# Two graph layers on one core: gathers for padding left out, and the subtraction of the means moved to GpSimd

## What is computed

```python
def layer0(x, src, dst):
    msg = concatenate([x[dst], x[src] - x[dst]])
    h = leaky_relu(msg @ W1 + b1, 0.01)
    h = leaky_relu(h @ W2 + b2, 0.01)
    return segment_sum(h, dst)

def layer1(x, src, dst):          # with a loop at every node
    y = (x @ W).reshape(N, 4, 64)
    logits = leaky_relu(sum(y * att_src)[src] + sum(y * att_dst)[dst], 0.2)
    alpha = softmax of logits over the edges of one dst
    return segment_sum(y[src] * alpha, dst).mean(heads) + bias

x = layernorm(x + layer0(x, src, dst))
x = layernorm(x + layer1(x, src, dst))
```

## Time and profile before

| | |
|---|---|
| median of 3 runs | 8135.93 us (8133.81 to 8150.75) |
| profiled execution | 8149.11 us |
| its span, first to last instruction | 8147.3 us |
| mean granted TensorE clock | 0.894 |
| busy: PE, DVE, ACT, POOL | 5916.5, 5650.8, 3861.1, 5850.7 us |
| gathers of the first layer | 3088, starts 95.1 to 3951.2 us |
| norm and set-up between the layers | 3978 to 4066 us |
| gathers of the second layer | 3087, starts 4043.6 to 7917.4 us |
| last turn's end, end of the last norm | 8031, 8147 us |

### The profile page before, as it was taken

The page is one execution under the profiler, slowest core; times in us unless marked ns, Lnnn a source line. Parts: engine busy times, 40 slices in busy tenths (PEclk is TensorE's granted clock), DMA queues, the critical chain, the costliest instruction groups (busy, mean ns, idle before and its releaser), DMA issues.

```text
span 8147.3 us, 248848 instructions
## 1 busy us (share of the span) xinstructions
PE 5916.5 (73%) x46847; PEld 4536.0 (56%) x46848; DVE 5650.8 (69%) x13519; ACT 3861.1 (47%) x10093; POOL 5850.7 (72%) x6184
## 2 busy tenths in 40 slices
PE   6787788777778877877546666666666766767667
PEld 5555565555555655555435555555555555555556
DVE  5555555555555555555658888888888888888887
ACT  4444444444444444444324545444454544545443
POOL 4777777777777777777477777777777777777760
PEclk8999999999989999999778889888888988888887
DMA  4222222222222222222211111111111111111120
GB/s 112 41 41 41 41 41 42 42 41 41 41 41 41 41 42 41 42 41 41 36 32 31 32 32 31 32 31 32 31 32 32 31 32 31 32 32 31 32 27 17
DMA packets 299581, 306.84 MB, mean 38 GB/s; under 512 B 193032, under 2 KB 196726, under 8 KB 298632
## 3 DMA queue, kind: packets, MB, share of 16 engines
q0 software_dynamic: 197600, 261.23, 18.2%
q1 hardware_dynamic: 99476, 38.71, 2.1%
q10 hardware_dynamic: 2068, 3.20, 0.1%
HBM read 286.38 MB, written 16.30 MB: 37 GB/s over the span
## 4 chain that ended last, share of the span: by engine, by line
POOL 28%; issue 23%; PE 22%; DVE 9%; SPq 9%; DVEq 4%; ACT 2%; POOLq 2%; DMA 2%; ACTq 0%
POOL big L492 28%; PE pu L1093 9%; SPq L377 5%; PE ps L975 2%; PE pu L989 2%; SPq L373 2%; ACT ST L1213 2%; PE ps L1012 2%; PE pu L1023 2%; PE ps L1007 2%; POOLq L480 1%; DVE state L822 1%; DVE ps L764 1%; DVE Y L793 1%; DVEq L271 1%
## 5 line engine op out<-in xcount | busy, mean ns | idle before, releaser
L492 POOL DMA_INDIRECT big<-x_dram,idx x3087 | 2933.7, 950 | 1032.5 <-issue 1026.1
L492 POOL DMA_INDIRECT big<-q_dram,idx x3088 | 2916.0, 944 | 1034.3 <-issue 1027.0
L1093 PE MATMUL pu<-Y,S 128*128 128x265 f32 x7872 | 2305.4, 441 | 1059.3 <-DVE state L822 1057.6
L1093 PEld LDWEIGHTS pu<-Y,S 128*128 128x128 f32 x7872 | 1590.7, 213 | 1418.3 <-issue 1139.6
L793 DVE TENSOR_TENSOR Y<-big,ps 128x1040 f32<-128x1040 f32 x984 | 1214.7, 1234 | 387.9 <-PE pu L1093 280.0
L596 DVE TENSOR_TENSOR S<-ps,few 128x1024 f32 x978 | 1197.9, 1225 | 168.1 <-DVE few L591 123.8
L636 DVE TENSOR_TENSOR ps<-ps,rowX 128x512 f32<-128x512 f32 x491 | 343.6, 700 | 1320.6 <-ACT rowX L1224 1318.5
L1213 ACT COPY ST<-ps 128x1024 bf16<-128x1024 bf16 x489 | 494.9, 1012 | 1277.6 <-PE ps L975 1226.2
L989 PE MATMUL pu<-rowX,S 128*128 128x192 bf16 x3936 | 555.6, 268 | 445.7 <-SPq L397 400.0
L1296 ACT COPY ST<-ps 128x1024 bf16<-128x1024 bf16 x490 | 495.4, 1011 | 637.6 <-PE ps L1116 600.7
L989 PEld LDWEIGHTS pu<-rowX,S 128*128 x3936 | 382.0, 99 | 603.0 <-issue 515.0
(11 more groups left out here) (179 smaller groups left out, 8267.8 us busy)
## 6 DMA issues: line engine op xcount, KB each, us to landing
big<-x_dram SPq DMA_DIRECT2D x6272, 0.3 KB
big<-q_dram SPq DMA_DIRECT2D x6144, 0.4 KB
big<-q_dram,idx POOLq DMA_INDIRECT x3088
big<-x_dram,idx POOLq DMA_INDIRECT x3087
rowX<-flag_dram SPq DMA_DIRECT2D x196, 32.0 KB
x_dram<-big SPq DMA_DIRECT2D x7, 483.0 KB, 6.8
idx<-srcT_dram SPq DMA_DIRECT2D x98, 32.0 KB
dstc<-dstT_dram SPq DMA_DIRECT2D x98, 32.0 KB
```

Source lines behind the costliest of these rows:

```text
L492: nc.gpsimd.indirect_dma_start(o, None, x_dram if l else q_dram, bass.IndirectOffsetOnAxis(ap=idx[:, half, t:t + 1], axis=0)).then_inc(gat ...
L1093: last = t_.matmul(bank, Sf[:, t, :], Y[:, t, :], start=(t == 0), stop=(t == 7))
```

## The change

The turns are counted without the group of padding (STEPS is 488). In the last batch all engines run 7 groups and not 8, and GpSimd gathers 53 tiles and not 64 (in the second layer one of them is SP's); VectorE and SP wait for so many. `supers` can leave more than the last batch outside its loop, since VectorE has to know in the batch before which number to wait for: VectorE's last 3 batches of the second layer are now written out.

In the norm between the layers VectorE forms the mean and GpSimd subtracts it. VectorE forms three means ahead and not one: its order is now centre of c+2, spreads of c, logits of c-1, scale of c. The last norm stays as it was.

```diff
-STEPS = G + NB - 1
+STEPS = NG + NB - 1
+REST = NT - (NS - 1) * TS
+GREST = -(-REST // TG)
...
-        def supers(eng, body):
-
-            with eng.Fori(0, NS // 2) as q:
+        def supers(eng, body, rolled=NS // 2 * 2):
+
+            with eng.Fori(0, rolled // 2) as q:
                 body(q * 2, q, 0)
                 body(q * 2 + 1, q, 1)
-            if NS % 2:
-                body(NS - 1, NS // 2, 0)
+            for i in range(rolled, NS):
+                body(i, i // 2, i % 2)
+
+        def final(i):
+
+            return isinstance(i, int) and i == NS - 1
...
-                with self.eng.Fori(0, GS if between is None else GS - 1) as r:
+                with self.eng.Fori(0, GREST if final(i) else GS if between is None else GS - 1) as r:
                     self.group(l, i, r, turn, arrive)
...
             for l in range(2):
+                if l:
+                    for c in range(NCH):
+                        pool.wait_ge(meaned, c + 1)
+                        y = x0[:, c * BC:(c + 1) * BC, :]
+                        mm = mean[:, c * BC:(c + 1) * BC]
+                        nc.gpsimd.tensor_tensor(y, y, mm.unsqueeze(2).to_broadcast([P, BC, D]), ALU.subtract
+                                                ).then_inc(centred, 1)
...
-                    for r in range(GS):
+                    for r in range(GREST if final(i) else GS):
                         pool.wait_ge(L[l]["y1" if l else "z1"], free)
...
-                        for t in range(r * TG, r * TG + TG):
+                        for t in range(r * TG, min(r * TG + TG, REST) if final(i) else r * TG + TG):
...
                 link(v.tensor_reduce(mm, y, AX.X, ALU.add))
+                if base == 0:
+                    v.tensor_scalar(mm, mm, 1.0 / D, None, ALU.mult).then_inc(meaned, 1)
+                    return
...
-            centre(chunk_of(x0, 0), 0, 0)
+            for c in range(3):
+                centre(chunk_of(x0, c), c, 0)
             for c in range(NCH):
-                if c + 1 < NCH:
-                    centre(chunk_of(x0, c + 1), c + 1, 0)
+                if 3 <= c + 2 < NCH:
+                    centre(chunk_of(x0, c + 2), c + 2, 0)
                 spreads(c, 0)
...
-                dve.wait_ge(gath[half], q * (16 * (TS - 1)) + 16 * (TS - 1))
+                dve.wait_ge(gath[half], q * (16 * (TS - 1)) + 16 * ((REST if final(i) else TS) - 1))
...
-            supers(dve, steps1)
+            supers(dve, steps1, (NS - 2) // 2 * 2)
```

More of the change, by code:

```diff
@@ L232, in build @@
         sgp, sgv = sem("sg_pe"), sem("sg_dve")
+        meaned = sem("ln_meaned")
         centred, squared, spread, rooted, normed = [sem(f"ln_{n}") for n in "centred squared spread rooted normed".split()]
@@ L395, in landed @@
                         n = TG - 1
+                    if final(i):
+                        n = min(TG, REST - r * TG)
                     sp.wait_ge(slot[half][r], q * (16 * (TG if r < GS - 1 else TG - 1)) + 16 * n)
@@ L424, in chunk1 @@
                 sp.dma_start(idx[:, half, :], srcT_dram[:, ds(i * TS, TS)]).then_inc(idx_in[half], 16)
-                if not (isinstance(i, int) and i == NS - 1):
+                if not final(i):
                     row_numbers(1, i + 1, 1 - half)
@@ L878, in steps1 @@
                 dve.wait_ge(dst_in[half], (q + 1 + (NS - NS // 2 if half == 0 else NS // 2)) * 16)
-                last = isinstance(i, int) and i == NS - 1
+                last = final(i)
                 walk1.steps(1, i, turn1(half), between=None if last else lambda: arrived(i + 1, q + half, 1 - half))
@@ L1124, in steps1 @@
                 turn_maxima(i)
-                walk1.steps(1, i, turn, between=None if isinstance(i, int) and i == NS - 1 else lambda: turn_logits(i + 1))
+                walk1.steps(1, i, turn, between=None if final(i) else lambda: turn_logits(i + 1))
             prime(pe, 1, "stp ad U0 U1")
```

## The result

The changed kernel takes 8114.5 us, the median of 7 runs (8100.3 to 8119.4); beside it the kernel before took 8135.6 (7 runs, 8133.8 to 8150.8). The ratio is 0.9961, with a 95% interval of 0.9952 to 0.9970, which is 24 to 39 us less. The two medians are only 21.1 us apart, and that lies outside the interval. In a second session before had a median of 8144.4 in 21 runs and the changed kernel one of 8116.5, ratio 0.9959 (0.9945 to 0.9973), and these medians are 27.9 us apart. The profiled execution has a span of 8117.6 us against 8147.3, 29.7 us less.

The account below looks back on a forecast made before the run. GpSimd's gather list was taken to bound each layer, with VectorE's turns after the last batch; -17.5 + 0.6 - 4.8 - 1.8 - 6.4 = -29.9 us off the median 8135.9 gave 8106 us, range 8096 to 8122.

Parts of the forecast that it names:

- Part 1: End of first layer: 11 gathers fewer and PE taking the last real group earlier, -17.5 us (bounds -13.7 and -18.5).
- Part 2: Norm between the layers: start later by GpSimd's 2.0 us subtractions, +0.6 us; VectorE's relief counted as 0.
- Part 3: Second layer's last batch: VectorE's 4.78 us wait for gathers goes, -4.8 us, and a cold PE with it, -1.8 us.
- The cold PE: Second layer, behind the last batch's wait: first accumulation takes 2.06 us instead of 3.90, -1.8 us (bounds 0 and -2.1).
- Part 4: Second layer's last turns: one turn less, -6.4 us.
- Part 5: VectorE's last three batches of the second layer written out instead of one: 0, bounds -1 and +3 us.
- The signs: Trace checks, among them second layer's gathers starting 14 to 18 us earlier, VectorE waiting 2.6 us for PE, rounds 6.7 us.
- (a): Layer ends: the slow landing is not the padding's, so the first layer gains 13.7 us, not 17.5; 8110 us, chance 0.12.
- (b): Norm: shared port lock lets each GpSimd subtraction delay a VectorE scale, 7 x 2.0 = 14 us; 8120 us, chance 0.07.
- (c): Norm: VectorE limits the ring after all, so the norm gains 7.6 us; 8098 us, chance 0.05.
- (d): Norm: GpSimd becomes the bound above 6.73 us a chunk; 30 us won elsewhere used up at 11 us; chance 0.03.
- (e): Whole kernel: the change does not do what it says, for instance a stream still waits for padding; about 8136, chance 0.02.

Follow-up runs that it names:

- e3: Kernel before with the padding's source indices spread over different rows instead of all 0, all gathers and the last group kept; 8125.8 us, ratio 0.9982.
- e0: The changed kernel as it is, profiled and timed again; 8116.5 us (5 runs).
- e1: Changed kernel with VectorE subtracting the means between the layers in the old order, padding still left out; 8114.3 us, ratio to before 0.9965.
- e2: Kernel before with only the norm's part of the change, padding still gathered and run; 8142.1 us (11 runs), ratio 0.9998.
- e5: Kernel before with VectorE's last three batches of the second layer written out; ratio 1.0002, and 1.0001 when run again.
- e4: Changed kernel with only the padding's gathers left out, the last group and its turn still run; ratio to before 0.9972.
- e4b: The kernel of e4 run again; ratio to before again 0.9972.
- e6: Changed kernel with GpSimd doing three operations a chunk (subtract, add, subtract the means) instead of one; ratio to before 0.9961.
- e7: Changed kernel with GpSimd doing seven operations a chunk on the means instead of one; ratio to before 0.9993.
- e8: Changed kernel with ScalarE making the node-row copies between the layers and VectorE's bias addition later, bias read from PSUM; ratio to before 1.0022.
- e8b: The kernel of e8 run again; ratio to before 0.9984.

## Why the prediction was right

The direction and the range held, and so did the mechanisms of parts 1, 2 and 4; part 3 was right in kind, and part 5 overlooked a small gain. The median is 8.5 us above the forecast.

**What bounds the kernel: right.** Each layer ends as its list of gathers ends, and the padding's single row lands slowly (e3).

**Part 1, the first layer: right.** Forecast -17.5, measured -18.0, -16.5 (e0) and -18.3 (e1). PE was expected to take the last real group at 3943.0 and took it at 3943.28. The 0.2 us taken off for the last turns had the wrong sign: from that row to the end of the layer it is 17.1 us, and it was 17.65 before.

**Part 2, the norm: right, a term too large.** Forecast +0.6. A subtraction takes 1.69 us and not 2.0, so the first reciprocal is only 0.1 us later; e2 shows it alone. VectorE's wait was to grow to 2.6 us and grew to 2.05: its small scaling of line 705 (line 686 before) now takes 0.78 us instead of 0.17 in rounds where GpSimd subtracts. The relief was hidden, as forecast.

**Part 3, the last batch's arrival: right in kind, short in size.** The wait of 4.78 us went. From the first gather to the last copy it is 3873.9 us (e0 3874.7, e1 3872.9) against 3882.2, 8.3 less and not 4.8. In e3, where only the landing differs, it is 4.9 less. So 2.6 to 4.4 us more came from somewhere. The step that was too simple took VectorE's 7921.03 for fixed. In before, e2 and e3 VectorE is ready for the last copy 3877.2 to 3877.5 us after the first gather, and in the changed kernel, e0 and e1 3872.9 to 3874.7. So it isn't chance between runs of one kernel. These three have the shorter turns of the batches written out (e5). The five turns ahead of the last copy take 33.4 to 33.5 us in them, and 34.8 to 35.3 in the others. At the copy before it, batch 48's, VectorE waits 3.1 to 3.7 us for the list, and at most 0.4 in the others, so it had got ahead there too. Such a wait costs in turn. The copies of all batches show that VectorE waits for the list, comes out of the wait with a cold PE, is late for the next copy (4.1 to 5.3 us behind the batch's last gather instead of 2.7), and works that off over the next 2 to 6 batches. How the 2.6 to 4.4 us divide between the shorter turns and the place in this saw-tooth is not shown: no profile at 8140 us has written-out batches and the padding. The cold PE itself (forecast -1.8) is the 2.2 us by which e3's stretch from the last copy to the end of the turns, 102.7 us, is shorter than before's 104.9. PE's granted clock shows it: 0.50 from 7930 to 7934 us of before, behind the wait, and 1.00 in the same place of e3 (7917 to 7921).

**Part 4, the turn: right.** Forecast -6.4; e3 and e4, with 102.7 and 102.5 us, against 95.6 to 95.9 without it: -6.6 to -7.1 (e4b -6.2 to -6.5).

**Part 5, written-out code: within its bounds, but not 0.** It costs nothing (e5), and it gains: the pause ahead of a turn's first weighting is 0.17 us and not 0.29 to 0.42. The 0.97 against 1.10 us of the earlier trace rows had already shown such a difference, and I set it to 0. By the five turns above, this and the fewer waits for PE in them come to 1.3 to 1.9 us before the last copy.

**The sum.** The layers gave 35.6 us where 29.9 were forecast, and the last norm took back 5.9, of which the prediction had nothing. That the profiled executions differ by 29.7 us is thus partly luck: two misses of some 6 us cancel. What was off in the forecast is the last step, from the parts to the median. I took 29.9 us off 8135.9, which lay at the low end of what this kernel takes: 21 later runs of it have a median of 8144.4, from 8134 to 8150. The text saw that runs are 14 us apart, and put it in the range but not in the forecast. Taken off the low runs of before, 8134 to 8137, the sum gives 8104 to 8107, and three of the seven runs lie at 8100 to 8106; four lie higher. From 8144.4 the same sum gives 8114.5. That this is the measured median is luck, since the sum misses both the 5.7 us more of the layers and the last norm.

**The signs.** One of them says wrong: the first gathers of the second layer start 18.3 us earlier, and the bound was 18 (16.8 in e0, 18.8 in e1). The first layer gave 0.5 us more than its part, the norm's start cost 0.5 less, and the way from the first reduction to the first gather is 0.3 shorter. VectorE's wait was to be 2.6 us and is 2.05. The others came as written.

**The rivals.** (a) fell by e3, (c) by e2. (b) did not occur for the scales, but e6 shows its mechanism. (d) decides where it was put: at a chunk's work above a round, e7 with 13.0 us rounds. The 6.3 us that e7's rounds are above 6.7 cost 50 us, 8 for each and not 7, since the start is later too; by that estimate the 30 us won elsewhere would be used up at 10.5 us a chunk and not at 11. (e) did not occur.

## What to carry to other kernels

Work for padding costs more than its share when it points to one address: spread the padding's indices, or leave it out, and look for it at the end of a list that bounds a stage, where each item counts until another engine is the late one (13.7 us of gathers gave 8.3 in the second layer). Moving an operation to another engine gains nothing when the engine it leaves is not in the ring that sets the pace; the idle time before the ring's next link tells it beforehand. When some turns of a loop are written out, compare the pauses in them with those in the loop: small ones repeat every turn. For changes of 0.3% a median of three runs, or even of seven, isn't enough to subtract from: it was 8136 here, and 8144 in 21.

## What the runs showed of the hardware

- 128 reads of one row land slowly: 8.78 us from the start of the last gather, against 2.47 with spread rows. The DMA engines are busy 0.68 to 1.09 of the time at 20 to 25 GB/s, and 0.20 at 39 GB/s otherwise.
- GpSimd's subtraction of 128 x 896 elements takes 1.69 us, VectorE's 1.09. While it runs, a VectorE scaling of 14 elements with one input waits for its end: 3962.87 + 0.78 is when GpSimd's first one ends (3961.93 + 1.69 = 3963.62). I had expected this of operations with two inputs in SBUF only. The Trainium skill's page "SBUF — State Buffer" (Who interferes with whom) names `tensor_scalar` too, as an operation that can run in a mode with both ports; the rows agree.
- GpSimd's issue of a gather waits for some operations of VectorE: 7.03 us beside an addition with two inputs in SBUF, 0.95 beside the same addition with one of them in PSUM (e8); 5.91 beside VectorE's copies from SBUF to SBUF, 0.96 when ScalarE makes them.
- VectorE pauses 0.17 us ahead of a turn's first weighting in batches written out, and 0.29 to 0.42 in a hardware loop. In the kernels with the norm's part (after, e0, e2) every other batch of the loop has 0.41, in before, e1 and e3 all have some 0.3. No run tells the cause.
- In the profiles of e4 to e8b single matmuls of a layer stand some 2 us apart as long as gathers run, and at full pace without them. No run tells the cause.
